# Two small transfers of the first attention leave SyncE's queue and are issued by ScalarE

## The chip, the cores and the metric

The kernel runs on one core of one Trainium2 chip. The metric is the device time of one execution in microseconds; lower is better. A profile is of one execution and gives its span, from the first instruction's start to the last one's end.

## The reference, cut to what matters

Two transformer layers over x of 32 batches x 256 tokens x 128 features, in float32. Only the first attention is touched by the change:

```python
qkv = jnp.einsum('bsd,ed->bse', x, w_qkv)            # 16 heads of 8
q = _apply_rope(q, cos_emb, sin_emb); k = _apply_rope(k, cos_emb, sin_emb)
scores = jnp.einsum('bhqd,bhkd->bhqk', q, k) / jnp.sqrt(8)
attn = jax.nn.softmax(scores, axis=-1)
out = jnp.einsum('bhqk,bhkd->bhqd', attn, v)
x = _layernorm(x + out_projected, axis=-1)
```

Behind it come a feed-forward layer, a second attention and a second feed-forward layer, each with its own residual and normalisation.

## The kernel before, in words

The program has four stages, one per sublayer, and each goes over the 32 batches in steps. A step of the first attention is cut into 16 slots, one per head. The order on each engine is written out by hand: `step(i, on)` of an engine runs through the slots of batch i and does, at slots named in `Slots`, the small work of other batches (up to four ahead, two behind). The engines meet at semaphores alone.

For each head the scores are computed twice. In step i, slot s, TensorE computes

- the **second score** of batch i (`second_score`, L1072), into one of two banks. ScalarE takes the exponential of it (L879). It waits for the exponential of two slots before.
- the **first score** of batch i+1 (`first_score`, L1086), into one of three banks. VectorE takes the negated maximum of each row of it (L934, the *shifts*). The first score of slot 0 waits for `stacked[0]`, the landing of the first half of batch i+1's q and k; each first score also waits for the maximum that frees its bank: slot 1 of a step waits for that of slot 15 of the step before.

The shifts of 8 heads are turned by TensorE (L1006), copied by ScalarE into `shift_rows` (L785: for the upper half `shift_rows_out(i, 1)` in slot 2, for the lower half of the next batch `shift_rows_out(i+1, 0)` in slot 10), and then moved by a transfer of 4 KB into one row of `stack`, so that the second score has the shift in it (`shift_rows_in`, L589). The second scores of slots 0 and 8 wait for these transfers (`shifted[0]`, `shifted[1]`). These two transfers are what the change moves.

SyncE issues all other transfers of the step, in this order, and stands still at each wait:

1. `x_in` of batch i+4 (L642)
2. the wait for ScalarE's copy of slot 2, and the upper shift transfer (L589)
3. the ten transfers of `parts_out_in_stack_order(i+2)` (L609 to L612): the split q and k of batch i+2 to DRAM. GpSimd made these parts one step earlier.
4. the wait for ScalarE's copy of slot 10, and the lower shift transfer of batch i+1 (L589)
5. the wait until the ten have landed, and `stack_in(i+2)` (L622), twice: half 0 once slot 7 of step i is through on TensorE, half 1 once slot 15 is. They bring q and k back in the order of `stack`. Half 0 is what slot 0 of step i+1 waits for at L1086.

Beside the scores TensorE has in its stream: the product with the values by groups of four heads (L1024, behind the scores of slots 3, 7, 11 and 15), v, q, k and output projections (L1131, L1191, L1178), and transposes. In a step with nothing missing VectorE has between slot 14 and slot 15 the sum for y (L969) and a rotation (L942).

`wait_apart` is a wait against a count in a register that stands as an instruction of its own.

Of the kernel before, what the change touches and what calls it, by code (L numbers as in the profile page):

```python
# [30 lines left out]
TILE_ROWS = 64  # L31
SLOTS = TILE_ROWS // HD
SHIFT_ROW = HEAD_ROWS
# [46 lines left out]
def wait(eng, sem, count):  # L80

    if isinstance(count, int) and count <= 0:
        return
    eng.wait_ge(sem, count)


def wait_apart(eng, sem, count):


    if not isinstance(count, int):  # L90
        count = eng.to_reg(count)
        eng.wait_ge(sem, 1)
    wait(eng, sem, count)


def wait_for_x(sp, before, writes, b, name="x_ready"):


    if isinstance(b.half, int):
        sp.wait_ge(before.sems[name], (b.number() + 1) * writes)  # L100


class Phase:
# [8 lines left out]
    def sem(self, name):  # L112
        self.sems[name] = self.core.sem(f"{name}_{self.name}")
        return self.sems[name]
# [23 lines left out]
def times(i, k, n):  # L138

    if isinstance(i.half, int):  # L140
        return max(0, min(n, 2 * i.half + i.odd + k + 1))
    assert i.first + i.odd + k >= 0, "no wait in a loop is for less than one"
    return i.half * 2 + (i.odd + k + 1)
# [303 lines left out]
def attention(nc, core, layer, banks, scratch, ctx, x_dram=None, before=None):  # L447
# [9 lines left out]
    n = core.n  # L457
    first = layer == 0
# [4 lines left out]
    b = [core.bank[k] for k in banks]  # L463
# [5 lines left out]
    slots = Slots(first)  # L469
# [3 lines left out]
    def sb(name, shape, dt=FP32):  # L473
        return ctx.enter_context(nc.sbuf_tensor(f"{name}_{layer}", shape, dt))
# [11 lines left out]
    shift_rows = [sb(f"shift_rows{k}", [half_heads, TOK], BF16) for k in range(2)]  # L486
# [45 lines left out]
    shift_rows_ready = sem("shift_rows_ready")  # L532
    shifted = [sem(f"shifted{k}") for k in range(2)]
# [43 lines left out]
    def stack_rows(parity, rows=HEAD_ROWS):  # L577
        return slice(parity * TILE_ROWS, parity * TILE_ROWS + rows)

    @phase.engine("sync")  # L580
    def _(sp):
        source = x_dram.rearrange("b (t p) d -> b p t d", p=P) if first else None

        def shift_rows_in(b, hf):


            wait_apart(sp, shift_rows_ready, b.number() * 2 + (hf + 1))
            rows = core.stack[b.odd][SHIFT_ROW:SHIFT_ROW + TILE_ROWS + 1:TILE_ROWS, 1, 4 * hf:4 * hf + 4, :]
            sp.dma_start(rows.rearrange("q r n -> q (r n)"), shift_rows[hf][:, :]).then_inc(shifted[hf], 16)  # L589

        def parts_out(b):

            for s, m in RUNS:
                k = K_PART[s]
                src = parts[b.odd][:, k:k + 1, sides - 1, :]
                if m > 1:
                    src = src.broadcast_to([P, m, TOK])
                sp.dma_start(scratch[b.odd, 0, s:s + m, :, :].rearrange("s r n -> r s n"), src).then_inc(parts_written, 16)
                sp.dma_start(scratch[b.odd, 1, s:s + m, :, :].rearrange("s r n -> r s n"),
                             parts[b.odd][:, Q_PART[s]:Q_PART[s] + m, 0, :]).then_inc(parts_written, 16)  # L600

        def parts_out_in_stack_order(b):

            for parity in range(2):
                split = parts[b.odd][parity * TILE_ROWS:(parity + 1) * TILE_ROWS, :, :, :]
                for s, m in RUNS[:2]:
                    q = K_PART[s]
                    to = scratch[b.odd, :, parity, s:s + m, :, :].rearrange("e s r n -> e r s n")
                    sp.dma_start(to[0], split[:, 0:m, 1, :]).then_inc(parts_written, 16)  # L609
                    sp.dma_start(to[1], split[:, q:q + 1, 0, :].broadcast_to([TILE_ROWS, m, TOK])).then_inc(parts_written, 16)  # L610
                k_and_q = split.rearrange("p k e n -> p (k e) n")[:, 1:5:3, :]
                sp.dma_start(scratch[b.odd, :, parity, USED - 1, :, :].rearrange("e r n -> r e n"), k_and_q).then_inc(parts_written, 16)  # L612

        def stack_in(b, i, on, hf):

            if on(0):

                wait_apart(sp, s_in_psum, i.number() * HEADS + half_heads * (hf + 1))
            prs = slice(4 * hf, 4 * hf + 4)
            if first:  # L620
                src = scratch[b.odd].rearrange("e a s (d r) n -> e (a s d) r n", r=PAIRS)[:, :, prs, :]
                sp.dma_start(core.stack[b.odd][:, :, prs, :].rearrange("p e r n -> p e (r n)"),  # L622
                             src.rearrange("e p r n -> p e (r n)")).then_inc(stacked[hf], 16)
                return
            for parity in range(2):
                for side, to in ((0, core.k_stack[b.odd][stack_rows(parity), prs, :]),
                                 (1, core.q_stack[b.odd][stack_rows(parity), prs, :])):
                    src = scratch[b.odd, side, :, parity * 64:(parity + 1) * 64, :].rearrange(
                        "s (d r) n -> s d r n", r=PAIRS)[:, :, prs, :].rearrange("s d r n -> s d (r n)")
                    sp.dma_start(to.rearrange("q r n -> q (r n)"), src).then_inc(stacked[hf], 16)  # L630

        def step(i, on):
            if on(4):
                b = i.plus(4)
                if before:
                    wait_for_x(sp, before, TILES, b, "xh_ready")

                wait_apart(sp, xt_in_psum, times(i, 2, n))
                if first:
                    wait_apart(sp, added_ready, times(i, 2, n))  # L640
                src = source[b.number(), :, :, :] if first else core.xh_all[:, b.number(), :, :]
                sp.dma_start(x_in[b.odd][:, :, :], src).then_inc(x_loaded[b.odd], 16)  # L642
            if on(0):
                shift_rows_in(i, 1)
            if on(2):
                b = i.plus(2)
                wait_apart(sp, parts_ready, times(i, 2, n))

                wait_apart(sp, stacked[0], times(i, 0, n) * (16 * reads))
                wait_apart(sp, stacked[1], times(i, 0, n) * (16 * reads))  # L650
                if first:
                    parts_out_in_stack_order(b)
                else:
                    parts_out(b)
            if on(1):
                shift_rows_in(i.plus(1), 0)
            if on(2):
                wait_apart(sp, parts_written, times(i, 2, n) * (16 * writes))
                stack_in(i.plus(2), i, on, 0)
                stack_in(i.plus(2), i, on, 1)  # L660

        return step
# [116 lines left out]
    def _(act):  # L779
# [26 lines left out]
        def norm(b, ts=range(TILES)):  # L806

            act.wait_ge(rstd_ready, b.number() + 1)
            act.wait_ge(norm_shift_ready, b.number() + 1)
            for t in ts:  # L810
                act.activation(core.x_all[:, b.number(), t, :], y_of(b)[:, t, :], ACT.Identity, scale=rstd[:, t:t + 1],
                               bias=norm_shift[:, t:t + 1]).then_inc(x_ready, 1)
# [15 lines left out]
        def step(i, on):  # L828
            for s in range(HEADS):
# [10 lines left out]
                if first and s == slots.v + 2 and on(1):  # L840
                    b = i.plus(1)
# [18 lines left out]
                if s == slots.xt + (1 if first else 0) and on(slots.xt_ahead):  # L860
                    b = i.plus(slots.xt_ahead)
# [10 lines left out]
                if on(0):  # L872
                    act.wait_ge(s_in_psum, i.number() * HEADS + (s + 1))

                    if first and s % 4 == 0:
                        wait(act, pv_done, i.number() * groups + (s // 4 - 1))
                    if not first:
                        wait(act, pv_done, i.number() * HEADS + (s + 1 - RING))
                    act.activation(probs[:, s % RING, :, :].rearrange("p t n -> p (t n)"), s2[s % 2][:, :], ACT.Exp,  # L879
                                   scale=scale).then_inc(exp_done, 1)  # L880
                if first and s == HEADS - 1 and on(-2):
                    norm(i.plus(-2), (1,))
                if not first and s == slots.norm and on(-1):
# [900 lines left out]
def build(nc, x, weights, out):  # L1784
# [5 lines left out]
    with ExitStack() as ctx:  # L1790
# [3 lines left out]

        places = [ExitStack() for _ in range(5)]
        attn0 = attention(nc, core, 0, (0, 1, 2, 3, 4, 5, 6, 7), in_stack_order, places[0], x_dram=x)
        early, middle, late = prepare(nc, core, w, in_stack_order, places[1])
        places[1].close()
        ffn0_ = ffn0(nc, core, attn0, places[2])
        places[0].close()  # L1800
        attn1 = attention(nc, core, 1, (2, 3, 5, 0, 7, 1, 4, 6), by_slot, places[3], before=ffn0_)
        places[2].close()
        ffn1_ = ffn1(nc, core, out, attn1, places[4])
# [44 lines left out]
```

## Time and profile before

| | |
|---|---|
| median of 3 runs | 1552.67 us (1552.26 to 1553.35) |
| profiled execution | 1553.82 us, span 1551.6 us |
| first attention in the span | from about 37 to about 530 us |
| busy share of the span | PE 95%, DVE 77%, ACT 68%, POOL 62% |
| `x_in`, parts, `stack` and shift transfers of the first attention | all on SyncE's queue |

PE is TensorE's matrix product, PEld its weight load, DVE VectorE, ACT ScalarE, POOL GpSimd, SP SyncE; SPq and ACTq are instructions that the engine's sequencer runs, such as the issue of a transfer. TensorE's busy time counts overlapping records once and their ends are modelled, so a busy share near 1 still hides short waits. What limits a stage is read from who waits for whom at a given place, not from the shares.

### The profile page before, as it was taken

The numbers are of one execution on the slowest core, as the hardware profiler recorded it, in microseconds if no ns is written. First come the engines' busy times: TensorE is split into PE (matmuls) and PEld (weight loads), VectorE is DVE, ScalarE is ACT, GpSimd is POOL, SyncE is SP. The second block draws the span as 40 slices with busy tenths as digits, with TensorE's granted clock in tenths as the row PEclk, the third lists the DMA queues.
The fourth block names the chain that finished last, engine by engine and source line by source line (L and its number), as shares of the span: only waits on it lengthen the run. The fifth ranks groups of instructions, "written<-read, shape, count | busy, mean of one in ns | idle before, by whom it ended". The sixth has DMA issues, their size and how long they took to land. (4 is left out here: it accounts for less than half of the span.)

```text
span 1551.6 us, 55296 instructions
## 1 busy us (share of the span) xinstructions
PE 1467.2 (95%) x17642; PEld 1145.0 (74%) x17642; DVE 1187.8 (77%) x3338; ACT 1051.0 (68%) x2581; POOL 966.2 (62%) x1160
## 2 busy tenths in 40 slices
PE   5999999999999799979999999999999999998998
PEld 3444555554554399959888888888888888997997
DVE  4777888888888478887878888788878887864666
ACT  2466777777778788856767777777777777774332
POOL 4555565655654067777778877887788777852222
PEclk8799999999999999979999999999999999999999
DMA  5344544454454100122222222222222222200111
GB/s 144 101 131 119 136 128 134 127 136 132 131 136 117 45 32 30 43 87 76 78 72 78 80 76 76 79 80 77 73 81 80 78 70 82 77 23 28 64 64 51
DMA packets 174124, 133.93 MB, mean 86 GB/s; under 512 B 13787, under 2 KB 145126, under 8 KB 174054
## 3 DMA queue, kind: packets, MB, share of 16 engines
q1 hardware_dynamic: 172944, 132.37, 29.4%
q8 instruction: 40, 0.66, 0.2%
q10 hardware_dynamic: 1110, 0.66, 0.1%
q14 instruction: 30, 0.25, 0.0%
HBM read 64.82 MB, written 55.05 MB: 77 GB/s over the span
## 5 line engine op out<-in xcount | busy, mean ns | idle before, releaser
L934 DVE TENSOR_REDUCE shifts<-bank 128x2 bf16<-128x512 f32 x1024 | 684.4, 688 | 169.7 <-PE bank L1086 166.0
L879 ACT ACTIVATE probs<-bank 128x512 f32<-128x512 f32 x1024 | 573.6, 594 | 139.6 <-PE bank L1072 138.2
L1034 PE MATMUL bank<-values,probs 64*128 64x129 f32 x8192 | 579.6, 277 | 3.8 <-DVE o_even L901 0.7
L1034 PEld LDWEIGHTS bank<-values,probs 64*128 64x128 f32 x8192 | 527.1, 188 | 30.6 <-issue 10.8
L1086 PE MATMUL bank<-stack 48*128 48x256 bf16 x2048 | 367.8, 277 | 38.8 <-DMA stack<-score_parts 20.6
L1072 PE MATMUL bank<-stack 49*128 49x256 bf16 x2048 | 376.4, 274 | 8.5 <-ACT probs L879 3.1
L680 POOL TENSOR_TENSOR values<-mix,v_in 128x1024 f32<-128x1024 f32 x128 | 302.0, 2361 | 0.0
L1072 PEld LDWEIGHTS bank<-stack 49*128 49x128 bf16 x2048 | 166.1, 95 | 140.8 <-ACT probs L879 90.2
L689 POOL TENSOR_TENSOR o_odd<-o_odd,scaled 128x256 f32<-128x256 f32 x224 | 163.3, 729 | 161.4 <-ACT scaled L803 161.1
L1086 PEld LDWEIGHTS bank<-stack 48*128 48x128 bf16 x2048 | 156.4, 96 | 61.8 <-DVE shifts L934 24.4
L803 ACT ACTIVATE scaled<-bank,recips 128x128 f32<-128x128 f32 x448 | 137.6, 357 | 88.7 <-DVE recips L928 88.7
L901 DVE SCALAR_TENSOR_TENSOR o_even<-bank,recips,o_even 128x128 f32<-128x128 f32 x448 | 136.7, 347 | 7.9
L1024 PE MATMUL bank<-probs,values 128*32 128x256 f32 x2048 | 139.4, 390 | 0.0
L928 DVE RECIPROCAL recips<-bank 128x2 f32<-128x2 f32 x512 | 84.9, 166 | 62.3 <-PE bank L1034 53.0
L705 POOL TENSOR_TENSOR shifted_var<-moments,ln_shift 128x2 f32<-128x2 f32 x64 | 12.5, 196 | 168.5 <-DVE moments L984 158.0
L1024 PEld LDWEIGHTS bank<-probs,values 128*32 128x32 f32 x2048 | 53.9, 110 | 50.8 <-issue 29.3
L758 POOL TENSOR_TENSOR exact<-turned 128x512 f32<-128x512 f32 x32 | 40.6, 1270 | 75.4 <-DVE turned L942 64.3
L1191 PE MATMUL bank<-x_t,w_qk 128*128 128x256 f32 x256 | 77.0, 428 | 1.4 <-ACT x_t L866 1.4
L1487 PE MATMUL bank<-w_proj,h_t_f 128*128 128x129 f32 x512 | 70.2, 281 | 2.3 <-issue 1.4
L1580 POOL TENSOR_TENSOR var_f<-moments_f,ln_shift 128x2 f32<-128x2 f32 x32 | 6.2, 195 | 102.7 <-DVE moments_f L1638 102.7
L1487 PEld LDWEIGHTS bank<-w_proj,h_t_f 128*128 128x128 f32 x512 | 63.5, 191 | 5.9 <-issue 4.1
L1602 ACT ACTIVATE gate_f<-bank 128x256 f32<-128x256 f32 x96 | 36.6, 383 | 43.5 <-PE bank L1660 43.3
(165 smaller groups left out, 2179.4 us busy)
## 6 DMA issues: line engine op xcount, KB each, us to landing
stack<-score_parts SPq DMA_DIRECT2D x64, 512.0 KB, 4.0
stack<-score_parts SPq DMA_DIRECT2D x256, 96.0 KB
score_parts<-parts SPq DMA_DIRECT2D x256, 64.0 KB, 2.1
score_parts<-parts SPq DMA_DIRECT2D x128, 96.0 KB, 2.3
score_parts<-parts SPq DMA_DIRECT2D x64, 192.0 KB, 2.3
x_in_f<-x_all SPq DMA_DIRECT2D x64, 128.0 KB, 2.0
score_parts<-parts SPq DMA_DIRECT2D x64, 128.0 KB, 2.3
x_in<-in_L_attn_x SPq DMA_DIRECT2D x32, 128.0 KB, 4.3
```

What stands on the lines that cost most here:

```text
L680: pool.tensor_tensor(values[i.plus(1).odd][:, t, heads, 0:D], core.mix[:, heads, :], v_in[:, t, :].unsqueeze(1).broadcast_to([P, half_head ...
L689: pool.tensor_tensor(o_odd[b.odd][:, :, :], o_odd[b.odd][:, :, :], scaled[:, h // 2 % 4, :, :], op=ALU.add).then_inc(odd_added, 1)
L803: act.activation(to, pv_bank(h)[:, t * (D + 1):t * (D + 1) + D], ACT.Copy, scale=recips[:, h % 2, t:t + 1]).then_inc(scaled_ready, 1)
L879: act.activation(probs[:, s % RING, :, :].rearrange("p t n -> p (t n)"), s2[s % 2][:, :], ACT.Exp, scale=scale).then_inc(exp_done, 1)
L901: dve.scalar_tensor_tensor(o_even[b.odd][:, t, :], part, recips[:, h % 2, t:t + 1], o_even[b.odd][:, t, :], op0=ALU.mult, op1=ALU.add).the ...
L928: dve.reciprocal(recips[:, h % 2, :], sums).then_inc(recips_ready, 1)
L934: dve.tensor_reduce(shifts[:, :, hf, col], s1_bank(s)[:, :].rearrange("p (t n) -> p t n", t=TILES), op=ALU.max, axis=AX.X, negate=True).th ...
L1024: last = pe.matmul(pv[0][VW * a:VW * (a + 1), 0:TOK], values[b.odd][:, t, :, :].rearrange("p h c -> p (h c)")[:, start:start + VW], probs[ ...
L1034: return pe.matmul(pv_bank(h)[:, q * (D + 1):(q + 1) * (D + 1)], probs[rows, h % RING, t, q * P:(q + 1) * P], values[b.odd][rows, t, h, :] ...
L1072: score = pe.matmul(s2[s % 2][:, t * TOK:(t + 1) * TOK], core.k_stack[b.odd][rows, s // 2, t * P:(t + 1) * P], core.q_stack[b.odd][rows, s ...
L1086: score = pe.matmul(s1_bank(s)[:, t * TOK:(t + 1) * TOK], core.q_stack[b.odd][rows, h // 2, t * P:(t + 1) * P], core.k_stack[b.odd][rows, ...
L1487: pe.matmul(out_banks[i.odd][:, t * width:t * width + D + 1], h_t[i.odd][:, c, own], core.w0_proj[:, c, :], start=(c == 0), stop=(c == chu ...
```

## The change

In the first attention ScalarE issues the two shift transfers on its own queue, each behind the exponential of the slot in which it copied the rows: the upper one behind slot 2's, the lower one behind slot 10's. SyncE no longer has them or their waits. The second attention keeps them on SyncE.

```diff
+    def shift_rows_in(eng, b, hf):
+
+        wait_apart(eng, shift_rows_ready, b.number() * 2 + (hf + 1))
+        rows = core.stack[b.odd][SHIFT_ROW:SHIFT_ROW + TILE_ROWS + 1:TILE_ROWS, 1, 4 * hf:4 * hf + 4, :]
+        eng.dma_start(rows.rearrange("q r n -> q (r n)"), shift_rows[hf][:, :]).then_inc(shifted[hf], 16)
+
     @phase.engine("sync")
     def _(sp):
         source = x_dram.rearrange("b (t p) d -> b p t d", p=P) if first else None
-
-        def shift_rows_in(b, hf):
-
-
-            wait_apart(sp, shift_rows_ready, b.number() * 2 + (hf + 1))
-            rows = core.stack[b.odd][SHIFT_ROW:SHIFT_ROW + TILE_ROWS + 1:TILE_ROWS, 1, 4 * hf:4 * hf + 4, :]
-            sp.dma_start(rows.rearrange("q r n -> q (r n)"), shift_rows[hf][:, :]).then_inc(shifted[hf], 16)
...
-            if on(0):
-                shift_rows_in(i, 1)
+            if not first and on(0):
+                shift_rows_in(sp, i, 1)
...
-            if on(1):
-                shift_rows_in(i.plus(1), 0)
+            if not first and on(1):
+                shift_rows_in(sp, i.plus(1), 0)
...
+                if first and s == slots.shifts1 and on(0):
+                    shift_rows_in(act, i, 1)
+                if first and s == slots.shifts0 and on(1):
+                    shift_rows_in(act, i.plus(1), 0)
```

SyncE's issues in an even step of the loop, before: `x_in0` is batch i+4's input, `score_parts0` the DRAM copy of batch i+2, `stack0` and `stack1` the two buffers of q and k; ISA and REGISTER_ALU are register work.

```order
L642 DMA x_in0_0<-in_L0_attn_x 128x2x128
L91 ISA
L589 DMA stack0<-shift_rows1_0 2x4x256
L91 ISA
L609 DMA score_parts0<-parts0_0 64x3x256
...
L612 DMA score_parts0<-parts0_0 64x2x256
L91 ISA
L589 DMA stack1<-shift_rows0_0 2x4x256
L91 REGISTER_ALU
L91 ISA
L622 DMA stack0<-score_parts0 128x2x1024
```

The same place on SyncE with the change:

```order
L641 DMA x_in0_0<-in_L0_attn_x 128x2x128
L91 ISA
L608 DMA score_parts0<-parts0_0 64x3x256
...
L611 DMA score_parts0<-parts0_0 64x2x256
L91 REGISTER_ALU
L91 ISA
L621 DMA stack0<-score_parts0 128x2x1024
```

Both shift transfers and the waits ahead of them are gone, so that the first of the ten parts stands directly behind `x_in`.

ScalarE in the same step, around slot 2 and around slot 10, before (`bank3` and `bank4` hold the second scores of even and odd slots):

```order
L785 ACTIVATE shift_rows1_0<-bank6 8x256
L879 ACTIVATE probs_0<-bank3 128x512
L879 ACTIVATE probs_0<-bank4 128x512
L790 ACTIVATE heads_t0_0<-bank5 128x256
...
L785 ACTIVATE shift_rows0_0<-bank6 8x256
L879 ACTIVATE probs_0<-bank3 128x512
L857 ACTIVATE o_t_0<-bank7 128x256
L879 ACTIVATE probs_0<-bank4 128x512
```

And with the change:

```order
L784 ACTIVATE shift_rows1_0<-bank6 8x256
L878 ACTIVATE probs_0<-bank3 128x512
L584 DMA stack1<-shift_rows1_0 2x4x256
L878 ACTIVATE probs_0<-bank4 128x512
L789 ACTIVATE heads_t0_0<-bank5 128x256
...
L784 ACTIVATE shift_rows0_0<-bank6 8x256
L878 ACTIVATE probs_0<-bank3 128x512
L584 DMA stack0<-shift_rows0_0 2x4x256
L856 ACTIVATE o_t_0<-bank7 128x256
L878 ACTIVATE probs_0<-bank4 128x512
```

The issue now stands between the exponentials of slots 2 and 3, and between the exponential of slot 10 and the copy of `o_t`, ahead of the exponential of slot 11.

## Rows read from the trace of the kernel before

**Rows 1.** Groups by line, 161.50 to 476.21 us, one `o_t` copy a step: busy, mean ns.

```profile
L857 ACT ACTIVATE o_t<-bank 128x256 f32<-128x256 f32 x21 | 7.5, 356 | 0.0
```

**Rows 2.** Timeline of PE, around slot 0 of one step: start, length, idle before.

```profile
311.02 0.28 PE L1072 MATMUL bank<-stack 49*128 49x256 bf16 x1
312.25 0.28 PE L1086 MATMUL bank<-stack 48*128 48x256 bf16 x1 [0.95 <-DVE shifts L934]
```

**Rows 3.** Timeline of SP, one step of 15 us and the next stack half.

```profile
296.20 0.38 SPq L642 DMA_DIRECT2D x_in<-in_L_attn_x  x1
299.09 0.58 SPq L589 DMA_DIRECT2D stack<-shift_rows  x1
299.98 0.63 SPq L609 DMA_DIRECT2D score_parts<-parts  x1
...
308.18 2.36 SPq L622 DMA_DIRECT2D stack<-score_parts  x2
```

**Rows 4.** Waits of SP's queue, 200 to 440 us (16 steps): total, times, longest.

```profile
SPq L84 <- ACT shift_rows L785: 39.0, 16, 2.7
```

**Rows 5.** Timeline of DVE: the maximum of slot 15, ahead of slot 1.

```profile
311.47 0.69 DVE L934 TENSOR_REDUCE shifts<-bank 128x2 bf16<-128x512 f32 x1
```

**Rows 6.** Timeline of PE: the second score of slot 0, in eight steps.

```profile
81.83 0.28 PE L1072 MATMUL bank<-stack 49*128 49x256 bf16 x1
...
99.29 0.28 PE L1072 MATMUL bank<-stack 49*128 49x256 bf16 x1
...
128.76 0.28 PE L1072 MATMUL bank<-stack 49*128 49x256 bf16 x1
...
146.65 0.28 PE L1072 MATMUL bank<-stack 49*128 49x256 bf16 x1
...
161.50 0.28 PE L1072 MATMUL bank<-stack 49*128 49x256 bf16 x1
...
490.55 0.28 PE L1072 MATMUL bank<-stack 49*128 49x256 bf16 x1
...
504.02 0.28 PE L1072 MATMUL bank<-stack 49*128 49x256 bf16 x1
...
521.79 0.29 PE L1072 MATMUL bank<-stack 49*128 49x256 bf16 x2
```

**Rows 7.** Waits, 80 to 133 us: PE at L1086 for the stack.

```profile
PE bank L1086 <- DMA stack<-score_parts: 4.9, 3, 2.2
```

**Rows 8.** Timeline of PE: the wait in the step that starts at 504.02.

```profile
507.57 0.28 PE L1086 MATMUL bank<-stack 48*128 48x256 bf16 x1 [3.27 <-DMA stack<-score_parts]
```

**Rows 9.** Timeline of SP: the stack halves ahead of that wait.

```profile
503.68 0.88 SPq L622 DMA_DIRECT2D stack<-score_parts  x2
```

**Rows 10.** Stage row: length, busy PE, PEld, DVE, ACT, POOL, granted clock, DMA.

```profile
508.53:511.94 3.41, 3.41 (x29) 1.28 (x27) 2.20 (x6) 1.91 (x4) 1.19 (x4) 0.50 0.00 1
```

**Rows 11.** Timeline, first 5 us: two issues by ACT, of four rows each.

```profile
1.21 0.57 ACTq L281 DMA_DIRECT2D raw_rows<-in_L_ffn_ln_w  x1
...
1.82 0.26 ACTq L282 DMA_DIRECT2D raw_rows<-in_L_ffn_ln_b  x1
```

**Rows 12.** Timeline of ACT, slot 2 and slot 10 of one step.

```profile
300.02 1.09 ACT L879 ACTIVATE probs<-bank 128x512 f32<-128x512 f32 x2 [1.01 <-PE bank L1072]
301.27 0.38 ACT L790 ACTIVATE heads_t<-bank 128x256 f32<-128x256 f32 x1 [0.17 <-PE bank L1024]
...
305.84 0.36 ACT L785 ACTIVATE shift_rows<-bank 8x256 bf16<-8x256 bf16 x1
306.11 0.57 ACT L879 ACTIVATE probs<-bank 128x512 f32<-128x512 f32 x1
306.58 0.36 ACT L857 ACTIVATE o_t<-bank 128x256 f32<-128x256 f32 x1
306.85 0.57 ACT L879 ACTIVATE probs<-bank 128x512 f32<-128x512 f32 x1
```

**Rows 13.** Timeline of PE: the second score of slot 13 in that step.

```profile
307.65 0.27 PE L1072 MATMUL bank<-stack 49*128 49x256 bf16 x1
```

## The prediction

> **What bounds the kernel now.** I first read the groups by line: a stretch of 314.71 us inside the first attention holds 21 `o_t` copies, one a step, so 21 steps of 14.99 us on average [rows 1]. TensorE is busy nearly all the time there, so what counts is where its stream stands still. The timeline of PE shows one place in each step: slot 0. The second score starts at 311.02 and the first score, which is issued beside it, at 312.25 [rows 2]. Between them TensorE has nothing to do: 256 columns at 2.4 GHz are an estimated 0.11 us, so about 1.1 us are lost. The view names VectorE as the releaser, but the first score of slot 0 needs the maximum of slot 14, and the one that runs at that time is slot 15's, as the next part shows. The other semaphore it waits for is the landing of the first half of `stack`. SyncE issued that at 308.18 [rows 3], 4.07 us before TensorE went on. So the landing ends this wait, and the releaser's name is a coincidence of time.
>
> Why does SyncE issue it so late? Its timeline [rows 3] shows `x_in` at 296.20, then nothing until the shift transfer at 299.09, and the first of the ten parts at 299.98. From there to the stack half are 8.2 us of issuing and landing. The waits of SyncE's queue give the reason: 39.0 us in 16 steps, 2.4 us a step, for ScalarE's copy of the shifts [rows 4]. The parts stand behind that wait, though GpSimd makes them in the step before.
>
> **What limits slot 1 next.** The first score of slot 1 needs the maximum of slot 15. It ends at 311.47 + 0.69 = 312.16 [rows 5], so with the landing gone the wait moves one slot on and is nearly as long. From 312.25 back to 312.16 and the two pairs of matmuls that are then already done, 2 x 0.11 us, are all that a usual step can win, 0.1 to 0.3 us. The shortest step of the loop shows the same floor: 146.65 to 161.50 is 14.85 us, the average 14.99 [rows 1, 6].
>
> But some steps lose more. 81.83 to 99.29 is 17.46 us and 128.76 to 146.65 is 17.89 [rows 6]. Between 80 and 133 us TensorE waited 4.9 us in three places for the stack, 2.2 at the longest [rows 7]. And at the end the step of 504.02 lasts 17.77 us where the one ahead of it lasts 13.47 [rows 6]: there TensorE waits 3.27 us for the stack [rows 8], whose issue at 503.68 stands 0.34 us ahead of the step that needs it [rows 9], and right after that the granted clock is 0.50, the lower of its two levels (1.2 GHz), for 3.41 us [rows 10].
>
> **The change part by part.**
>
> *SyncE without the two transfers.* `x_in` ends at 296.58; with about 0.3 us of register work, as between the shift transfer's end (299.67) and the first part (299.98), the parts start near 296.9 and not 299.98: 3.1 us earlier [rows 3]. The stack half follows 8.2 us behind, at 305.1; slot 7, its other condition, is through at about 303.5, estimated from slot 0 a step ahead of 311.02, at 296.0, and half a step. It lands at 305.1 + 4.1 = 309.2, and slot 0 of the next step is at 311.02 [rows 2]: 1.8 us to spare. Gains, in the profiled execution:
>
> - 21 usual steps: 14.99 - 14.85 = 0.14 us each, 2.9 us.
> - The two long ones near the start: 17.46 - 14.85 = 2.6 and 17.89 - 14.85 = 3.0, 5.6 us. Their landings were about 1.2 us later than usual, which the 3.1 us cover.
> - The last two: here slot 15 has no rotation ahead of it, so no wait takes the place of the landing. I take 12.3 us for a clean step, 13.47 less a wait like the 1.2 us of a usual step. 13.47 - 12.3 = 1.2 and 17.77 - 12.3 = 5.5, 6.7 us, of which up to 1.7 (half of 3.41) are the clock.
>
> Together 15.2 us.
>
> A rule of the Trainium skill speaks against this part: "DMA: Bandwidth & Descriptors", section "Issuing engines are not separate DMA queues", says that issuing from several engines saves only the sequencer's time for the issue. By it SyncE wins two issues of 0.58 us, 1.2 us a step, the usual wait still goes but the wait of 3.27 us keeps about 2 us; the sum would be some 2 to 3 us smaller. The rows show a wait in the queue, not only an issue, so I take theirs.
>
> *ScalarE with the two transfers.* No row shows a small issue of this shape on ScalarE. Its issues of four rows at the program's start took 0.57 and 0.26 us [rows 11], SyncE's of this very transfer 0.58 [rows 3]. I take 0.58, as the nearest in shape.
>
> Slot 10: the issue must wait for the copy, which ends at 305.84 + 0.36 = 306.20, runs until about 306.85, and then the `o_t` copy starts at 306.9 and not 306.58, and the exponential of slot 11 at 307.17 and not 306.85 [rows 12]. It ends at 307.74 and not 307.42. The second score of slot 13 waits for it and runs at 307.65 today [rows 13], 0.23 us after it; with the exponential 0.32 us later and a few hundredths for the semaphore it comes 0.15 us late. Behind it TensorE's stream has no pause until slot 0, so the step is that much longer; 0.17 taken.
>
> Slot 2: the exponentials of slots 2 and 3 start at 300.02 and, 1.09 - 0.60 later, at 300.51. With the issue and 0.2 us of register work between them the second starts at about 300.85. The next, the copy of the heads, stands at 301.27 behind an idle time of 0.17 for TensorE [rows 12]; it could now start at 300.85 + 0.49 = 301.34. So 0.07 to 0.2 us late, 0.13 taken, and the exponentials of slots 4 and 5, for which slots 6 and 7 wait, with it. The more so as SyncE is issuing its parts at that time.
>
> Together 0.30 us a step, over 30 steps 9.0 us. Bounds: nothing, if the issue takes 0.26 us (the spare time at slot 13, some 0.17, and at the heads, 301.27 - 301.00 = 0.27, then nearly cover it); and 1.1 us a step, 33 us, if ScalarE's issue only starts when the exponential ahead of it has ended (0.6 us later in slot 2, 0.5 in slot 10). I take the middle way because ScalarE starts its operations 0.49 us apart although each lasts 0.60 [rows 12]: its sequencer does not wait for an end.
>
> *Moved transfers.* The upper shifts are issued 1.1 us later than now (300.2 for 299.09), the lower ones earlier; slots 8 and 0 need them over 4 us later. Nothing.
>
> *The sum.* Against the profiled execution (1553.8 us, 1.1 above the median): -15.2 + 9.0 = -6.2 us. Against the median 1552.7: 1546.5 us. No change that is under 0.2%, 3.1 us, can be told from none.
>
> **The rivals.**
>
> *The issue on ScalarE is hidden* (0 to 0.1 us a step). For it: the two spare times. Then 1552.7 - 15.2 + 0 to 3 = 1537.5 to 1540.5. The Trainium skill, "Perfetto Trace Analysis", section "DVE / Act Engine Instruction", has the sequencer push an operation into a wait queue and go on; by that the issue of slot 2 would run in the 1.01 us in which its exponential waits. No view here lists what the sequencer does then. Chance 0.15.
>
> *ScalarE becomes the bound* (slower). One mechanism: the issue holds ScalarE's stream longer than 0.58 us, since it waits for the exponential's end or for SyncE's issues, which now fill slots 1 to 8. It decides from 0.5 us a step, where it eats the 15.2. At 0.6 to 1.1 us a step the time is 1552.7 - 15.2 + 18 to 33 = 1555.5 to 1570.5. Against it: at the start ScalarE's issues kept to 0.57 and 0.26 us [rows 11] while SyncE issued its own. The skill's same page, section "DMA Instruction — HWDGE (DVE, Sync)", has one descriptor generator locked by one sequencer at a time, which would add up to SyncE's 0.6 us in slot 2. Chance 0.11.
>
> *The long steps stay long.* The landings of parts slip to another place, or the tail is held by VectorE or the feed-forward stage. Then the gain is 2.9 to 10 us against 9.0 of cost: 1551.7 to 1558.8. For it: nothing in the rows says what delayed the landings in the two steps near the start. Chance 0.24, a third of it over +3 us.
>
> **How the numbers follow.** The forecast itself has 0.50, with a range of its own of 1543 to 1550 (0.18 to 0.42 us a step). Faster by over 0.2%, under 1549.6: nearly all of the 0.50, the 0.15, a little of the last: 0.66. Slower, over 1555.8: 0.11 and a part of the last, 0.16. Between: 0.18. The range for 8 in 10 leaves out the lower end of the first rival and the upper of the other two: 1539 to 1555.
>
> **What would show it.** On SyncE the first part 0.3 us behind `x_in`, the stack half near 9 us behind it. On PE no wait for the stack at slot 0, one of 0.9 us at slot 1 named after VectorE's shifts. The usual step 15.1 to 15.2 us long, longer than now, and slot 13 and slots 6 and 7 0.1 to 0.2 us later in it. No step over 16 us from 81 us on, and no clock of 0.50 near 508 us. ScalarE's issues 0.58 us long. The forecast is wrong if those issues are much shorter or longer, if the usual step stays at 14.9 or passes 15.4, or if a step of 17 us remains.

## The result and the profile after

The changed kernel takes 1543.57 us (median of 5 runs, 1540.85 to 1547.2), the kernel before in the same comparison 1552.67 us (1552.26 to 1554.32). The ratio is 0.994, with a 95% interval of 0.9921 to 0.9959: about 9 us faster. The profiled execution of after took 1546.57 us (span 1544.5), 7.25 us less than that of before.

Groups by line of after, over a stretch of 21 steps (busy, mean ns, idle before). Each of the seven rows behind it, from the timeline of PE, is the second score of slot 0 in one step.

```profile
L856 ACT ACTIVATE o_t<-bank 128x256 f32<-128x256 f32 x21 | 8.1, 383 | 3.6 <-issue 3.6
```

```profile
82.79 0.28 PE L1075 MATMUL bank<-stack 49*128 49x256 bf16 x1
...
97.57 0.28 PE L1075 MATMUL bank<-stack 49*128 49x256 bf16 x1
...
157.72 0.28 PE L1075 MATMUL bank<-stack 49*128 49x256 bf16 x1
...
474.11 0.28 PE L1075 MATMUL bank<-stack 49*128 49x256 bf16 x1
...
488.30 0.28 PE L1075 MATMUL bank<-stack 49*128 49x256 bf16 x1
...
500.56 0.28 PE L1075 MATMUL bank<-stack 49*128 49x256 bf16 x1
...
514.09 0.40 PE L1075 MATMUL bank<-stack 49*128 49x256 bf16 x4
```

Set beside [rows 1, 6], these starts cut the two spans into the same five stretches:

| stretch, by slot 0 | before | after | difference | forecast |
|---|---|---|---|---|
| start to the 3rd batch | 81.83 | 82.79 | +0.96 | +0.3 |
| the next 5 steps | 79.67 | 74.93 | -4.74 | -4.1 |
| 21 usual steps | 314.71 | 316.39 | +1.68 | +3.4 |
| the last 3 steps | 45.58 | 39.98 | -5.60 | -5.8 |
| all behind them | 1029.8 | 1030.4 | +0.6 | 0 |

The usual step is *longer* than before: 316.39 / 21 = 15.07 us against 14.99. The kernel is faster because the few long steps are gone. 82.79 to 97.57 is 14.78 us where before took 17.46, and the last step, 500.56 to 514.09, is 13.53 us where it was 17.77.

What SyncE does in a step now, from the timeline of SP:

```profile
293.51 0.38 SPq L641 DMA_DIRECT2D x_in<-in_L_attn_x  x1
294.20 0.59 SPq L608 DMA_DIRECT2D score_parts<-parts  x1
...
302.46 5.44 SPq L621 DMA_DIRECT2D stack<-score_parts  x2
```

The first part is issued 0.69 us behind the start of `x_in`, where it was 3.78 [rows 3]. The `stack` half follows 8.95 us behind `x_in` and not 11.98. The waits of SP's queue over the same 16 steps as in [rows 4] (total, times, longest) no longer name ScalarE's copy:

```profile
SPq L84 <- PE bank L1075: 73.0, 16, 4.6
```

This is the wait of the second half of `stack` for slot 15: SyncE now stands still there for about 4.6 us in every step (73.0 / 16). On PE the timeline around slot 0 shows where the wait of [rows 2] went:

```profile
308.38 0.28 PE L1075 MATMUL bank<-stack 49*128 49x256 bf16 x1
308.38 0.28 PE L1089 MATMUL bank<-stack 48*128 48x256 bf16 x1
...
309.57 0.28 PE L1089 MATMUL bank<-stack 48*128 48x256 bf16 x1 [0.69 <-DVE shifts L937]
```

The first score of slot 0 starts with the second score. The first score of slot 1 then waits for the maximum of slot 15, 1.19 us behind slot 0, so the step wins almost nothing. From 80 us on, only in the last step is the landing still late, as the timeline of PE shows. From 507 to 512 us the granted clock is 1.00, where [rows 10] had 0.50.

```profile
501.24 0.28 PE L1089 MATMUL bank<-stack 48*128 48x256 bf16 x1 [0.41 <-DMA stack<-score_parts]
```

The timeline of ACT holds both new issues (ACTq), in slot 2 and in slot 10:

```profile
297.16 0.60 ACT L878 ACTIVATE probs<-bank 128x512 f32<-128x512 f32 x1 [1.01 <-PE bank L1075]
297.23 0.52 ACTq L584 DMA_DIRECT2D stack<-shift_rows  x1
297.86 0.60 ACT L878 ACTIVATE probs<-bank 128x512 f32<-128x512 f32 x1
298.42 0.38 ACT L789 ACTIVATE heads_t<-bank 128x256 f32<-128x256 f32 x1
...
302.99 0.36 ACT L784 ACTIVATE shift_rows<-bank 8x256 bf16<-8x256 bf16 x1
303.25 0.57 ACT L878 ACTIVATE probs<-bank 128x512 f32<-128x512 f32 x1
303.43 0.52 ACTq L584 DMA_DIRECT2D stack<-shift_rows  x1
303.99 0.38 ACT L856 ACTIVATE o_t<-bank 128x256 f32<-128x256 f32 x1 [0.17 <-issue]
304.27 0.59 ACT L878 ACTIVATE probs<-bank 128x512 f32<-128x512 f32 x1
```

Slot 13's second score in that step and the last matmul of its first score, from the timeline of PE:

```profile
304.92 0.28 PE L1075 MATMUL bank<-stack 49*128 49x256 bf16 x1
...
305.12 0.27 PE L1089 MATMUL bank<-stack 48*128 48x256 bf16 x1
```

and the same last matmul in the step of [rows 13], before the change:

```profile
307.76 0.27 PE L1086 MATMUL bank<-stack 48*128 48x256 bf16 x1
```

In slot 2 the second exponential starts 0.70 us behind the first where it took 0.49, but the copy of the heads stands 1.26 us behind the first, where it stood 1.25 [rows 12]: it waited for TensorE anyway, and nothing is late. In slot 10 the `o_t` copy and the exponential of slot 11 start 0.74 and 1.02 us behind slot 10's exponential, where they took 0.47 and 0.74 [rows 12]. That is 0.28 us late, and TensorE feels it: the step is 15.07 - 14.85 = 0.22 us longer than the clean one. From slot 13 to the next slot 0 it takes 308.38 - 304.92 = 3.46 us, where it took 311.02 - 307.65 = 3.37 [rows 2, 13]. So 0.13 of the 0.22 are lost up to slot 13's second score and 0.09 from there on. These 0.09 lie inside slot 13 itself: this last matmul starts 0.20 us behind the second score (305.12 - 304.92), where it took 0.11 (307.76 - 307.65), and from there to the next slot 0 both kernels take 3.26 us. The `o_t` copy has no part in it: it ends at 304.37, and the output projection that reads it starts at 305.32, 0.20 us behind this matmul, as before (307.96 and 307.76).

### The profile page after: what moved, and what is told of

The parts are those of the page before. It is cut to its first block and busy times, and to the rows that moved or that the text cites. A ratio compares the mean times of both kernels' runs of the same rounds, so it can differ in the third digit from the quotient of the medians.

```text
span 1544.5 us, 55248 instructions
## 1 busy us (share of the span) xinstructions
PE 1471.5 (95%) x17642; PEld 1140.9 (74%) x17642; DVE 1185.6 (77%) x3338; ACT 1060.6 (69%) x2581; POOL 966.2 (63%) x1160
## 5 line engine op out<-in xcount | busy, mean ns | idle before, releaser
L878 ACT ACTIVATE probs<-bank 128x512 f32<-128x512 f32 x1024 | 580.5, 595 | 115.8 <-PE bank L1075 109.6
L1089 PE MATMUL bank<-stack 48*128 48x256 bf16 x2048 | 381.0, 277 | 29.5 <-DVE shifts L937 23.8
L1075 PEld LDWEIGHTS bank<-stack 49*128 49x128 bf16 x2048 | 162.1, 95 | 149.4 <-ACT probs L878 71.7
L1089 PEld LDWEIGHTS bank<-stack 48*128 48x128 bf16 x2048 | 151.6, 95 | 53.5 <-DVE shifts L937 38.3
```

The source lines that it names most:

```text
L1075: score = pe.matmul(s2[s % 2][:, t * TOK:(t + 1) * TOK], core.k_stack[b.odd][rows, s // 2, t * P:(t + 1) * P], core.q_stack[b.odd][rows, s ...
L1089: score = pe.matmul(s1_bank(s)[:, t * TOK:(t + 1) * TOK], core.q_stack[b.odd][rows, h // 2, t * P:(t + 1) * P], core.k_stack[b.odd][rows, ...
```

## The experiments

Three theories stood at the start. **Queue**: the gain is that the ten parts no longer stand behind SyncE's wait for ScalarE's copy, and the cost is the issue behind slot 10's exponential alone. **Issue time**: the gain is only the time of two issues that SyncE no longer makes. **ScalarE**: any issue on ScalarE costs the step, in slot 2 as in slot 10. Each time is the median of 5 to 12 runs, for the kernel before once more that of one; the kernel before took 1553.02 us in the first four's comparison (17 runs, 1545.86 to 1557.41) and 1551.58 us in the last four's (15 runs, 1548.28 to 1554.32).

**The changed kernel once more** (no edit).

> The changed kernel once more, as the yardstick beside the three others. Theory A (mine): the gain is the stack half that SyncE issues 3 us earlier, the cost is ScalarE's issue in slot 10, which makes the exponential of slot 11 and with it slot 13 late, 0.22 us a step. Usual step 15.07 us as in the first profile, 1541 to 1547 us. The spread of its five times against that of the kernel before should be explained by how long the granted clock is 0.50 at the start, where the first profile had it until 64.2 us against 61.4 before.

Measured: 1542.98 us, ratio 0.9939 (0.9919 to 0.9959). The gain repeats, and with it the usual step of 15.07 us and a last step of 13.26 us. Its step of the first batch is 17.96 us long, as in the profile of before, and not 18.53 as in the one of after, and its granted clock is 0.50 until 60.4 us and not 64.15. The start explains about half of the spread: the two spans differ by 3.8 us (1544.5 and 1540.7), of which 1.7 lie ahead of the third batch (slot 0 at 81.05 and 82.79) and 1.8 behind the first attention.

**SyncE keeps both transfers, in another order.** The upper one goes between the fifth and the sixth part, the lower one between the two halves of `stack`; ScalarE issues nothing.

```diff
                 if first:
-                    parts_out_in_stack_order(b)
+                    parts_out_in_stack_order(b, (0,))
...
+            if first and on(0):
+                shift_rows_in(i, 1)
+            if first and on(2):
+                parts_out_in_stack_order(i.plus(2), (1,))
...
                 stack_in(i.plus(2), i, on, 0)
+            if first and on(1):
+                shift_rows_in(i.plus(1), 0)
+            if on(2):
                 stack_in(i.plus(2), i, on, 1)
```

> From the kernel before. SyncE keeps both shift transfers, but issues the upper one behind the first five of the ten parts and the lower one between the two stack halves, so that it stands at neither wait; ScalarE issues nothing. Theory A: all of the gain and none of the cost: no wait for the stack at slot 0, usual step 14.85 us against 15.07, so 0.22 x 28 = 6 us below the changed kernel, about 1537. Theory B (rival): the transfers gain because they run on a queue of their own beside the parts, or because SyncE is rid of their issue time; then this kernel stays at 1547 or above and the usual step at 14.95 or more.

Measured: 1539.26 us, ratio 0.9907 (0.9887 to 0.9926). Rows of its timelines, PE's slot 0 in two steps that follow each other, and SP's first issue of the shifts ahead of them (the second is at 300.66):

```profile
305.10 0.28 PE L1079 MATMUL bank<-stack 49*128 49x256 bf16 x1
...
319.94 0.28 PE L1079 MATMUL bank<-stack 49*128 49x256 bf16 x1
```

```profile
294.57 0.57 SPq L589 DMA_DIRECT2D stack<-shift_rows  x1
```

SyncE still pays for both issues, 0.57 us each, and the step is 14.85 us. So issue time is not what counted: the order of the queue is. This kernel, with one queue, is faster than the changed one with two.

**The lower transfer one exponential later.** ScalarE issues it behind the exponential of slot 11.

```diff
-                if first and s == slots.shifts0 and on(1):
+                if first and s == slots.shifts0 + 1 and on(1):
                     shift_rows_in(act, i.plus(1), 0)
```

> From the changed kernel: ScalarE issues the lower shift transfer behind the exponential of slot 11, ahead of an idle time of 0.5 us, and not behind that of slot 10. Theory A: the exponential of slot 11 is on time again, slot 13 with it, usual step 14.85 us, 1537 to 1538 us. Theory C (rival): any issue on ScalarE costs its stream, wherever it stands, or the one in slot 2 is what costs; then the step stays at 15.0 to 15.1 and the time at 1543.

Measured: 1538.38 us, ratio 0.991 (0.9892 to 0.9928), the shortest of all. Its slot 0 in two steps on PE, and ACT around slot 10:

```profile
303.34 0.28 PE L1075 MATMUL bank<-stack 49*128 49x256 bf16 x1
...
318.18 0.28 PE L1075 MATMUL bank<-stack 49*128 49x256 bf16 x1
```

```profile
298.43 0.57 ACT L878 ACTIVATE probs<-bank 128x512 f32<-128x512 f32 x1
298.82 0.52 ACTq L584 DMA_DIRECT2D stack<-shift_rows  x1
...
299.17 0.57 ACT L878 ACTIVATE probs<-bank 128x512 f32<-128x512 f32 x1
```

The step is 14.85 us, and the exponential of slot 11 stands 0.74 us behind that of slot 10, as before the change. The issue stands behind it in the program and yet starts 0.35 us ahead of it: the sequencer had handed on both operations and went on. All that the issue of slot 10 cost, 15.07 - 14.85 = 0.22 us a step, is saved; the difference of the two medians is 4.6 us.

**The wait alone kept on SyncE.** As the changed kernel, but SyncE waits for ScalarE's copy of slot 2 ahead of the parts, without having a transfer to issue.

```diff
             if on(2):
                 b = i.plus(2)
+                if first and on(0):
+                    wait_apart(sp, shift_rows_ready, i.number() * 2 + 2)
                 wait_apart(sp, parts_ready, times(i, 2, n))
```

> From the changed kernel: SyncE issues neither transfer but still waits for ScalarE's copy of slot 2 ahead of the ten parts. So it is rid of issue time alone. Theory A: the stack half comes about 0.6 us earlier than before the change, not 3 us; usual step 15.07 us, bound by slot 13 as in the changed kernel, but the long waits in the last steps stay (over 1.5 us at 500 us) and the clock may fall there again: 1546 to 1550 us. Theory B (issue time is what counts): the same time as the changed kernel, 1543 to 1544, with no long step.

Measured: 1549.51 us, ratio 0.9983 (0.9968 to 0.9999). By the medians 6.5 of the 10 us that the change gives in this comparison are the wait. The split is rough: the interval of this kernel's ratio allows it a gain of 0.2 to 5.0 us. The waits of SP's queue, 16 steps, then the last step on PE and its stage row (length, busy PE, PEld, DVE, ACT, POOL, granted clock, DMA):

```profile
SPq L84 <- ACT shift_rows L786: 36.2, 16, 2.4
```

```profile
498.05 0.28 PE L1077 MATMUL bank<-stack 49*128 49x256 bf16 x1
501.76 0.28 PE L1091 MATMUL bank<-stack 48*128 48x256 bf16 x1 [3.44 <-DMA stack<-score_parts]
...
517.13 0.40 PE L1077 MATMUL bank<-stack 49*128 49x256 bf16 x4
```

```profile
503.00:506.30 3.30, 3.30 (x30) 1.56 (x29) 1.94 (x4) 1.78 (x4) 1.19 (x4) 0.50 0.05 14
```

The stall of 3.44 us and the clock of 0.50, the lower of the two levels, are back, and the last step is 19.08 us long (13.26 in the changed kernel's second profile). In the loop the step stays at 15.07 us, with the first score of slot 0 within 0.3 us of the second from the 8th to the 29th step: there the time of the two issues is enough. It is enough near the start too: the two long steps last 15.20 and 15.06 us here, the one behind them 15.43, with no clock of 0.50 in them. So the two causes share the work by place: the last step alone is 5.8 us longer than in the changed kernel's second profile.

**The kernel before once more**, in a single execution (no edit).

> This is the kernel before, profiled once more, to see which of its long steps belong to the kernel and which to one execution. If the late landings near 90 and 138 us and the stall near 508 us come from the order of SyncE's queue, two or three steps of 17 to 18 us stand again at the same places, the loop's steps last 14.85 to 15.1 us with slot 0's first score 0.95 to 1.25 us late, and the last step lasts over 17 us. If they are chance of one execution, a step of over 16 us is missing near 81 or 128 us or stands elsewhere, and then the gain of 5.6 us that the prediction took from these two steps is not a property of the kernel.

Measured: 1550.72 us. Second scores of slot 0 on PE, of the first long step:

```profile
79.69 0.28 PE L1072 MATMUL bank<-stack 49*128 49x256 bf16 x1
...
96.84 0.28 PE L1072 MATMUL bank<-stack 49*128 49x256 bf16 x1
```

The same three steps are long: 17.15, 17.86 (from 126.31 us) and 18.75 us (from 499.87). They belong to the kernel. The 21 usual steps last 14.91 us here and not 14.99, so that a usual step had only 0.06 us to win in this execution. What delays the first of them shows in the DMA view of before, between 76.8 and 79.5 us, ahead of the slot 0 at 81.83 (queue and kind: packets, MB, share of 16 engines; last column to landing, us):

```profile
q8 instruction: 1, 0.02, 3.3%
...
score_parts<-parts SPq DMA_DIRECT2D x1, 64.0 KB, 3.3
```

One packet of the kind `instruction`, program code, takes 3.3% of 16 engines x 2.7 us = 1.4 us on the DMA engines while the last part lands, and this part needs 3.3 us where 2.1 is usual for one of 64 KB. `stack` may only be fetched when all ten have landed. The second long step has such a packet ahead of it too (between 118 and 130 us), and the last one (at 501.06 us; the last part needs 2.9 us); the usual step at 180 to 190 us has none. Another stands between 91.5 and 94.5 us, with a last part of 2.7 us, and the step behind it is not long: the step of 17.46 us had given the queue time, and the part landed 3.8 us ahead of slot 0, where 3.0 is usual and the first long step had 1.9. Such packets are in the changed kernel too. One meets the last part at 134.4 us, which then needs 3.7 us, but it lands 4.6 us ahead of slot 0 and nothing waits. That the packet is the cause of the late landing is read from its place and time; no run took it away.

The late landing alone doesn't make 17 us: with the wait kept on SyncE the last part ahead of this step needs 3.65 us, no clock falls, and the step lasts 15.20. These are the stage rows of before inside this step (columns as above), ahead of and behind the end of the wait:

```profile
81.90:85.20 3.30, 1.25 (x13) 0.83 (x12) 2.07 (x5) 0.71 (x2) 0.00 (x0) 1.00 0.88 275
85.35:88.60 3.25, 3.25 (x15) 1.70 (x14) 0.94 (x4) 0.90 (x3) 1.20 (x4) 0.50 0.20 55
```

In the first TensorE is busy 1.25 of 3.30 us, in the second the granted clock is 0.50, as in [rows 10] after the wait of 3.27 us. The landing is 1.2 us later than usual and the wait as much longer (2.05 us idle where 0.6 to 0.95 is usual), and the clock behind it costs an estimated half of 3.25 at most, another 1.6. That is up to 2.8, and this step is 2.6 us over 14.85.

**The upper transfer alone on ScalarE**, behind slot 2's exponential. SyncE keeps the lower one where it was, behind the parts.

```diff
-            if on(0):
-                shift_rows_in(i, 1)
+            if not first and on(0):
+                shift_rows_in(sp, i, 1)
...
+                if first and s == slots.shifts1 and on(0):
+                    shift_rows_in(act, i, 1)
```

> ScalarE issues the upper transfer alone, behind slot 2's exponential; SyncE keeps the lower one and its wait behind the ten parts. Theory A (the gain is that SyncE's parts no longer stand behind the wait for the copy of slot 2; the cost is the issue behind slot 10 alone): no cost in slot 2, a usual step of 14.85 us, the stack half issued about 4 us ahead of slot 0 and landing in time, a last step of 13 to 14 us; 1538 to 1541 us, some 4 us less than the changed kernel. Theory B (each issue on ScalarE costs about half of the 0.22 us that a usual step lost): a usual step of 14.96 us, 1541 to 1544 us. Theory C (SyncE's lower issue and wait matter as much as the upper): the stack half lands late again at slot 0 and the last step stays over 16 us; 1545 us or more.

Measured: 1539.48 us, ratio 0.9921 (0.9908 to 0.9934). PE at slot 0 of two steps:

```profile
302.87 0.28 PE L1073 MATMUL bank<-stack 49*128 49x256 bf16 x1
...
317.72 0.28 PE L1073 MATMUL bank<-stack 49*128 49x256 bf16 x1
```

14.85 us: the issue in slot 2 costs nothing, and moving this one transfer gives more than moving both did (12.1 us against 10.0). Only the last step is a little longer than where both moved, 13.70 us, with its first score 1.01 us behind the second. The ScalarE theory falls.

**The lower transfer alone on ScalarE**, behind slot 10's exponential. SyncE keeps the upper one and its wait ahead of the parts.

```diff
-            if on(1):
-                shift_rows_in(i.plus(1), 0)
+            if not first and on(1):
+                shift_rows_in(sp, i.plus(1), 0)
...
+                if first and s == slots.shifts0 and on(1):
+                    shift_rows_in(act, i.plus(1), 0)
```

> ScalarE issues the lower transfer alone, behind slot 10's exponential; SyncE keeps the upper one, with its wait ahead of the parts. Theory A (cost is slot 10's issue, gain is the wait removed ahead of the parts): a usual step of 15.07 us or a little more, slot 13 at 11.61 us or later after slot 0, the stack half landing 0.1 to 1 us after slot 0, the wait of over 3 us and the clock of 0.50 near the last step still there; 1550 to 1556 us. Theory B (half of the cost each): a usual step of 14.96 us, 1547 to 1550 us. Theory C (the lower transfer matters as much): the last step comes down to about 15 us and the time to under 1547 us.

Measured: 1555.87 us, ratio 1.0028 (1.0017 to 1.0039), slower than before the change. Slot 0 and the first score on PE, the next step's slot 0, and the first score of the last step:

```profile
311.32 0.28 PE L1073 MATMUL bank<-stack 49*128 49x256 bf16 x1
...
312.09 0.28 PE L1087 MATMUL bank<-stack 48*128 48x256 bf16 x1 [0.49 <-DMA stack<-score_parts]
...
326.38 0.28 PE L1073 MATMUL bank<-stack 49*128 49x256 bf16 x1
...
508.79 0.39 PE L1087 MATMUL bank<-stack 48*128 48x256 bf16 x1 [3.76 <-DMA stack<-score_parts]
```

The step is 15.07 us long although the landing's wait is under 1 us, so that the length comes from slot 10 alone, and the long steps stay. This half of the change is all cost. (One of its ten runs took 3441 us; nothing explains it, and no other run did so.)

**The lower transfer behind the `o_t` copy**, ahead of the exponential of slot 11.

```diff
                     act.activation(o_t[:, :], m1[:, 0:TOK], ACT.Copy).then_inc(ot_ready, 1)
+                if first and s == slots.shifts0 + 1 and on(1):
+                    shift_rows_in(act, i.plus(1), 0)
...
-                if first and s == slots.shifts0 and on(1):
-                    shift_rows_in(act, i.plus(1), 0)
```

> As the changed kernel, but ScalarE issues the lower transfer one operation later, between the o_t copy and the exponential of slot 11. It tells apart the two parts of the 0.22 us that the usual step lost: slot 13's second score 0.13 us late because of the exponential of slot 11, and 0.09 us more at slot 14 that I lay to the o_t copy, late for the output projection. If that is right, slot 13 stays 0.13 us late, the 0.09 us go, and the usual step lasts 14.98 us: about 1541.5 us, 2 us less than the changed kernel. If the whole 0.22 us come from the exponential of slot 11, the step stays at 15.07 us and the time at 1543 us. If both come from the o_t copy, the step is 14.85 us and the time 1538 us.

Measured: 1539.35 us, ratio 0.9918 (0.9904 to 0.9932). Slot 0 in two steps on PE, and ACT around slot 10:

```profile
307.66 0.28 PE L1075 MATMUL bank<-stack 49*128 49x256 bf16 x1
...
322.52 0.28 PE L1075 MATMUL bank<-stack 49*128 49x256 bf16 x1
```

```profile
317.34 0.36 ACT L784 ACTIVATE shift_rows<-bank 8x256 bf16<-8x256 bf16 x1
317.60 0.57 ACT L880 ACTIVATE probs<-bank 128x512 f32<-128x512 f32 x1
317.78 0.52 ACTq L584 DMA_DIRECT2D stack<-shift_rows  x1
318.08 0.36 ACT L856 ACTIVATE o_t<-bank 128x256 f32<-128x256 f32 x1
318.41 0.60 ACT L880 ACTIVATE probs<-bank 128x512 f32<-128x512 f32 x1
```

The step is 14.86 us and not 14.98, and slot 13 is not late. My split of the 0.22 us between the two operations fell. The issue starts 0.08 us behind the copy of the shifts' end (317.70), as it does in the changed kernel (303.35 and 303.43), since this is what it waits for. But one more operation was handed on ahead of it: the `o_t` copy starts while the issue runs, and the exponential of slot 11 comes 0.81 us behind that of slot 10, 0.07 late and not 0.28. This is within what slot 13 has to spare. With both on time the 0.22 us go at once, so this run alone doesn't tell which of them the last 0.09 us hung on. The changed kernel's own trace does, as shown above: its `o_t` copy ends 0.95 us before the output projection reads it, so it was never the one that was late, and the 0.09 us were lost between slot 13's own matmuls.

## Why the prediction was right, and where it was off

The forecast was 1546.5 us with a gain of 6.2; the median is 1543.57, and the profiled pair differs by 7.25. By its own steps:

- **What bounds the kernel.** Right. The landing ended the wait at slot 0, in spite of VectorE's name in the row, and it was late because the parts stood behind a wait for ScalarE. The kernel that keeps this wait shows it: 6.5 us slower, with the stall of the last step back. But it also shows that the two long steps near the start, which the prediction laid to that wait, went with the issue time alone. The queue that reorders both transfers and spares no issue gains more than the change did.
- **The wait that takes its place.** Right: slot 1 waits for the maximum of slot 15, and a clean step is 14.85 us, the floor that the shortest step gave. Four kernels have it. The usual steps could win only 0.14 us each, by the second profile of before 0.06.
- **The gains, 15.2 us.** Nearly right. The kernel that has them with no cost in the loop, the lower transfer behind slot 11, stands 14.6 us under the kernel before. In it the five steps near the start, two of them the long ones, gave 5.75 us (79.67 - 73.92) where 5.6 was reckoned, though about half of it was the clock and not the landing, which the prediction saw only at the end. The last step was mis-sized: 13.53 us and not 12.3. About 0.7 of this is its landing: the step ahead of it takes only 12.26 us, while SyncE needs 8.8 us for the parts and their landing, so that the `stack` half is issued at 496.64, 3.92 us ahead of slot 0, and the first score comes 0.68 us after it. The other 0.5 is the step itself, which is no copy of the one ahead of it: in the four kernels with the clean loop it lasts 12.88, 13.09, 13.31 and 13.70 us with its first score 0.19, 0.40, 0.61 and 1.01 us late, so 12.69 or 12.70 us without that in each, where the step ahead of it takes 12.15 to 12.36.
- **The cost, 0.30 us a step.** The step was 0.22 longer than the floor. The term for slot 2, 0.13, was wrong: it took the second exponential to start 0.83 us behind the first and to push the copy of the heads. It starts 0.70 behind, and the copy of the heads does not move. The term for slot 10, 0.17, was a little small: slot 13's second score is 0.13 us late, near the 0.15 reckoned, but another 0.09 goes between slot 13's own matmuls. The issue lasts 0.52 us; 0.58 was taken. So it is partly luck that the sum came as near as it did: one term stood for nothing, and the other was too small. Together 0.22 and not 0.30, which over 21 usual steps is the 1.7 us between the forecast's +3.4 and the +1.68 measured.
- **Start.** The forecast had only the +0.3 of the cost there. The profiled execution of after has a granted clock of 0.50 until 64.15 us where before it was back at 61.4, and the step of the first batch is 18.53 us and not 17.96. Other profiles, of before too, have 16.8 to 20.1 us for it. The changed kernel once more has 17.96, so it is no effect of the change.

The rule of the Trainium skill that spoke against the change ("DMA: Bandwidth & Descriptors", section "Issuing engines are not separate DMA queues": issuing from several engines saves only the sequencer's issue time) describes the kernel with the wait kept, in which exactly the two issues are saved. That one gained 1553.02 - 1549.51 = 3.5 us, near the 3 to 4 that the rule leaves of the predicted gain (6.2 less 2 to 3), and the change itself 10.0. The rest is a wait at the head of a queue, which the rule leaves out. The kernel with SyncE's queue reordered agrees with it in that no second queue was needed for the gain.

Of the rivals, the issue hidden on ScalarE did not happen in this kernel, and did in the one with the transfer behind slot 11: 1538.38 us, in the 1537.5 to 1540.5 that the prediction gave for it. ScalarE as the bound would have needed 0.5 us a step. The long steps did not stay.

## What to carry to other kernels

When a queue in order has a wait for another engine ahead of work that is ready, first reorder the queue: a small transfer that waits belongs behind the work that doesn't. A second queue is only another way to do this, and its issue goes where the issuing engine has operations already handed on, not right behind the one that everything waits for. Look for the gain in the few steps in which the late transfer meets a short step or another delay: the average wait of 1.2 us at slot 0 was worth next to nothing, as the next wait stood behind it, and the rare ones gave most.

## What the runs showed of the hardware

- ScalarE's sequencer runs ahead of its engine. With the transfer behind slot 11 its issue starts at 298.82, ahead of the exponential in front of it (299.17). But it did not pass an operation whose semaphore wasn't there yet: in slot 2 the copy of the shifts was long done, and the issue starts 0.07 us after the start of the exponential that had waited 1.01 us for TensorE. The Trainium skill, "Perfetto Trace Analysis", section "DVE / Act Engine Instruction", has an operation pushed into a wait queue and the sequencer go on to the next. The first row agrees, the second does not. Between the exponential and the issue stands the instruction of `wait_apart`, and the exponential waits for a count in a register; no run shows whether one of these holds the sequencer.
- An issue of the 4 KB transfer lasts 0.52 us on ScalarE and 0.56 to 0.58 on SyncE. ScalarE's at 297.23 overlaps two of SyncE's issues of parts, which stay 0.61 us long, but the next one, at 298.10, lasts 0.70, and in the following step 0.94. So it goes in every one of 16 steps: one part's issue, in two of them two, lasts 0.66 to 0.94 us, where before the change none passed 0.63. No step of the loop waits for it.
- One packet of program code on the DMA engines, 1.4 us, went with a landing that was 1.2 us later, and the steps that it met were 2.3 to 3.0 us longer before the change; with the change such a landing came 4.6 us ahead of its need and cost nothing.
- In each of the long steps the granted clock fell to 0.50, its level of 1.2 GHz, between 1.9 us before and 1.9 us behind the end of TensorE's wait for the stack. The waits were 1.4 to 3.8 us. It stayed there for 3.4 us, and for 6.8 us in the last step of three kernels: the one before in its second profile, the one with the wait kept and the one with the lower transfer alone. Behind the wait of 1.0 to 1.1 us one step ahead of the last it did not fall. What it cost in the last step is an estimate from the 12.69 us above (12.84 where the issue behind slot 10 is): the length less this and less the lateness of the first score is 1.5 us for 3.4 us at the low clock, and 2.2 to 2.5 us for 6.8.
